# Attention sums transposed by VectorE straight from their PSUM bank, without ScalarE's copy in SBUF

## The reference

```python
h = x @ W1 + b1                                   # q, k, v, 16 heads of 8
w = einsum('bhqd,bhkd->bhqk', q, k) / sqrt(8)
w = softmax(w * mask - (1 - mask) * 1e6)
a = einsum('bhqk,bhkd->bhqd', w, v)
x = layernorm(x + a @ Wp + bp)
xr, xk = mu * x + (1 - mu) * x_prev               # one mu each
x = layernorm(x + sigmoid(xr @ W_r.T) * (square(relu(xk @ W_k.T)) @ W_v.T))
```

## Time and profile before

| | |
|---|---|
| median of 3 runs | 651.06 us |
| the profiled execution's own time | 650.12 us |
| its span, first to last instruction | 648.4 us |
| busy PE, DVE, ACT, POOL | 564.7, 550.0, 451.1, 413.6 us |
| L736, the copy to `osum`, 32 times | 18.7 us on ACT |
| L860, the transposition, 32 times | 22.4 us on DVE |
| one step in the steady part (from 290.32 to 325.64 us) | 35.32 us |

### The profile page before, as it was taken

One profiled execution on the slowest core, in us unless ns is written; L12 is line 12 of the kernel. 1 busy time (PEld: TensorE's weight loads), 2 busy tenths in 40 slices (PEclk: granted clock), 3 DMA queues, 4 the chain that ended last, 5 costly groups with the idle time before them and its releaser, 6 DMA issues.

```text
span 648.4 us, 17196 instructions
## 1 busy us (share of the span) xinstructions
PE 564.7 (87%) x6438; PEld 243.9 (38%) x6438; DVE 550.0 (85%) x1579; ACT 451.1 (70%) x878; POOL 413.6 (64%) x576
## 2 busy tenths in 40 slices
PE   3457888999999999999999999999999999997864
PEld 1122333444343534343443444343434344342333
DVE  1477789999999999999999999999999999894437
ACT  2102777777787878787878778787878787776831
POOL 4100425667778686767767786867777777757673
PEclk9999999999999999999999999999999999997965
DMA  4652262525355443726264545436362535410101
GB/s 169 116 148 51 84 135 77 140 52 149 85 148 101 134 101 116 134 85 135 51 168 81 149 103 147 95 125 116 117 126 64 133 66 148 85 37 3 33 17 33
DMA packets 70825, 65.78 MB, mean 101 GB/s; under 512 B 14357, under 2 KB 60502, under 8 KB 70742
## 3 DMA queue, kind: packets, MB, share of 16 engines
q1 hardware_dynamic: 70178, 64.22, 41.2%
q10 hardware_dynamic: 564, 0.46, 0.3%
HBM read 34.70 MB, written 29.88 MB: 100 GB/s over the span
## 4 chain that ended last, share of the span: by engine, by line
PE 38%; DVE 28%; POOL 14%; ACT 7%; issue 6%; DMA 5%; SPq 2%; DVEq 0%; POOLq 0%; ACTq 0%
DVE rowmax L813 16%; PE ops L606 12%; PE sps L579 8%; POOL probs L1021 6%; PE tps L541 5%; PE spare L502 4%; POOL scaled L1059 4%; PE sps L564 4%; ACT probs L730 3%; POOL mixed L1063 3%; PE spare L482 3%; PE spare L516 2%; DMA d_parts<-qk_parts 2%; DVE stats L819 2%; DVE attnT L876 2%
## 5 line engine op out<-in xcount | busy, mean ns | idle before, releaser
L813 DVE TENSOR_REDUCE rowmax<-sps 128x1 f32<-128x512 f32 (+7 forms) x1024 | 395.6, 444 | 36.0 <-PE sps L579 34.7
L730 ACT ACTIVATE probs<-tps 128x512 f32<-128x512 f32 x640 | 347.6, 598 | 98.0 <-PE tps L541 95.4
L1021 POOL TENSOR_SCALAR_AFFINE_SELECT probs<-probs 128x512 f32<-128x512 f32 x256 | 158.6, 637 | 172.8 <-ACT probs L730 172.2
L606 PE MATMUL ops<-probs,vop 128*32 128x384 f32 (+3 forms) x2048 | 173.7, 446 | 15.9 <-ACT osum L736 8.1
L579 PE MATMUL sps<-kop,qop 48*64 48x512 bf16 (+7 forms) x2048 | 130.0, 309 | 12.1 <-DMA kop<-d_parts 12.1
L541 PE MATMUL tps<-qop,kop 50*128 50x384 bf16 (+3 forms) x1024 | 126.7, 306 | 12.3 <-ACT probs L730 11.6
L564 PE MATMUL sps<-qmask,dup 64*128 64x128 bf16 (+1 forms) x640 | 69.8, 215 | 28.2 <-DVE rowmax L813 25.9
L541 PEld LDWEIGHTS tps<-qop,kop 50*128 50x128 bf16 x1024 | 34.2, 94 | 147.7 <-ACT probs L730 122.8
L606 PEld LDWEIGHTS ops<-probs,vop 128*32 128x32 f32 x2048 | 50.4, 109 | 79.5 <-issue 41.5
L579 PEld LDWEIGHTS sps<-kop,qop 48*64 48x64 bf16 x2048 | 43.0, 106 | 53.4 <-issue 21.7
L564 PEld LDWEIGHTS sps<-qmask,dup 64*128 64x128 bf16 x640 | 31.3, 94 | 75.2 <-DVE rowmax L813 70.7
(11 more groups left out here) (111 smaller groups left out, 501.0 us busy)
## 6 DMA issues: line engine op xcount, KB each, us to landing
qop<-d_parts SPq DMA_DIRECT2D x64, 192.0 KB, 4.5
kop<-d_parts SPq DMA_DIRECT2D x63, 192.0 KB, 5.0
d_parts<-qk_parts SPq DMA_DIRECT2D x15, 768.0 KB, 3.4
d_parts<-qk_parts SPq DMA_DIRECT2D x15, 512.0 KB, 4.6
d_parts<-qk_parts SPq DMA_DIRECT2D x17, 256.0 KB, 4.6
xT<-x_by_channel SPq DMA_DIRECT2D x16, 256.0 KB, 2.6
xres<-x SPq DMA_DIRECT2D x16, 256.0 KB, 3.5
out<-result SPq DMA_DIRECT2D x15, 256.0 KB, 2.5
```

The source lines that it names most:

```text
L606: last = nc.tensor.matmul(ops[32 * t:32 * t + 32, BLK * a:SEQ], vop[:, par, a, QUARTET * half + t, hh, :], probs[:, g % 2, i, off:off + w] ...
L730: nc.scalar.activation(probs[:, g % 2, i, :], tps[:, bank(n), :], ACT.Exp, scale=SCALE)\
L813: last = nc.vector.reduce_max(rowmax[:, par, QUARTET * half + i, a:a + 1], sps[:, bank(n), off:off + w], axis=AX_X)
L1021: last = nc.gpsimd.affine_select(out=v, in_=v, compare_op=ALU.is_ge, fill=0.0, base=0, pattern=[[0, QUARTET], [1, BLK]], channel_multiplie ...
```

## The change

ACT's copy, its semaphore and `osum` are taken out. DVE transposes out of the PSUM bank itself, one group sooner (groups 6 and 1), behind the first two reductions of the group; it waits for `pv_done`, and `pv` waits for `turned_done`. The reciprocal becomes a function of its own, `invert`, which stays in groups 7 and 2. For half 0, `divide` moves from group 8 to group 7, right behind the reciprocal; for half 1 it stays in group 3.

```diff
-        osum = sb("osum", [P, 2, SEQ])
...
-                    wait(pe, o_copied, 2 * batch + half)
+                    wait(pe, turned_done, 2 * batch + half)
...
-            def copy_o(n, half):
-                wait(act, turned_done, 2 * n + half - 1)
-                wait(act, pv_done, GROUPS * n + CHUNKS * (half + 1))
-                nc.scalar.copy(osum[:, half, :], ops[:]).then_inc(o_copied, 1)
...
-                        if place == 0 and tg == 1 and active("D", tb):
-                            copy_o(before("D", tb), 1)
-                        if place == 0 and tg == CHUNKS + 1 and active("T", tb):
-                            copy_o(before("T", tb), 0)
...
             def turn_sums(n, half):
 
                 m = 2 * n + half
-                wait(dve, o_copied, m + 1)
+                wait(dve, pv_done, GROUPS * n + CHUNKS * (half + 1))
                 wait(dve, attn_done, m)
-                nc.vector.transpose(turned[:].rearrange("q b s h d -> q (b s h d)"), osum[:, half, :])\
-                    .then_inc(turned_done, 1)
+                nc.vector.transpose(turned[:].rearrange("q b s h d -> q (b s h d)"), ops[:]).then_inc(turned_done, 1)
+
+            def invert(n, half):
+                m = 2 * n + half
                 wait(dve, turned_done, m + 1)
                 nc.vector.reciprocal(inv[:, half], turned[:, :, 1, :, 0]).then_inc(inv_done, 1)
...
+                    if tg == 1 and active("D", tb):
+                        turn_sums(before("D", tb), 1)
+                    if tg == CHUNKS + 1 and active("T", tb):
+                        turn_sums(before("T", tb), 0)
                     for _, use, n in ORDER[b, g, 0]:
                         spare_use(use, n)
                     if tg == 2 and active("D", tb):
-                        turn_sums(before("D", tb), 1)
+                        invert(before("D", tb), 1)
                     if tg == 3 and active("D", tb):
                         divide(before("D", tb), 1)
                         turn_back(before("D", tb))
                     if tg == CHUNKS + 2 and active("T", tb):
-                        turn_sums(before("T", tb), 0)
-                    if tg == CHUNKS + 3 and active("T", tb):
+                        invert(before("T", tb), 0)
                         divide(before("T", tb), 0)
```

More of the change, by code:

```diff
@@ L296, in block_program @@
         pv_done = sem("pv_done")
-        o_copied = sem("o_copied")
         turned_done = sem("turned_done")
```

## The result

The changed kernel takes 661.15 us, the median of 4 runs (658.49 to 663.85), against 650.67 for the kernel before beside it (4 runs, 649.69 to 652.81): a ratio of 1.016, with an interval of 1.011 to 1.021. It is slower, as forecast, but by 10.5 us where 2.95 were forecast, and it lies above the range. The profiled execution took 661.99 us, 11.87 more than that of before.

The account below looks back on a forecast made before the run. PE (33.50) and DVE (33.39 of 35.32 us per step) share the bound. 6.75 us lost, 2.80 and 1.0 gained: 651.06 + 2.95 = 654.0 us, range 649.0 to 657.5.

Parts of the forecast that it names:

- 15 x 0.45 = 6.75: Groups 6 and 7, half 0: group 8's first mask 0.45 us late in each of 15 steps, 6.75 us lost.
- `h` 0.51: DVE in groups 6 and 7: `h` behind the transposition takes 0.51 us, the same as before the change.
- ACT's copies: 32 copies of 0.58 us on ACT, which has 7 us to spare per step: removal counted at nothing beside the scores.
- The product in group 7: Half 0's product, moved from group 8, adds 0.41 us to DVE's work in group 7 and gives nothing back.
- PE's wait before `pv`: Group 6: `pv` starts 0.79 us later, behind the transposition; PE gets part back, leaving some 0.04 us.
- PE gets nothing back: Rival: PE sets the pace behind group 6, so 0.79 us are lost per step; 659.1 us, chance 0.07.
- Group 1 and 2: Half 1: group 2 is rid of the transposition, some 0.20 us gained per step, 14 times, 2.80 us.
- The price of the transposition: DVE transposing out of PSUM takes 0.70 us, as from SBUF, with 0.65 and 0.75 as the ends.
- the rival of a dearer one: Rival: the transposition out of PSUM takes 0.75 us, so both waits grow; 655.5 us, chance 0.13.
- Behind the last scores: After the last scores, DVE's transposition replaces the copy while DVE is idle: 1.0 us gained, bounds 0 and 1.0.
- the 0.62 us: Last batch's chain from `pv` over the transposition to its projection: shorter by a copy and a hand-over, some 0.62 us.

Follow-up runs that it names:

- `h_last`: The changed kernel with the second half of the layer norm (`h`) moved behind group 6's last two reductions; 653.89 us, ratio 1.003 to before.
- `masks_after_h`: The changed kernel with POOL's masks of group 6 waiting until `h` is done, DVE's order untouched; 652.41 us, ratio 1.000 to before.
- `idle_copy`: The changed kernel with an added ACT copy in group 6, in the old copy's place, that nothing reads; 657.69 us, one run.
- `product_g8`: The changed kernel with half 0's product put back from group 7 into group 8; 656.37 us, ratio 1.007 to before.
- `both_moved`: The changed kernel with half 0's product back in group 8 and `h` behind group 6's last two reductions; 650.5 us, ratio 0.999 to before.
- `turn_between`: The changed kernel with product back in group 8, `h` behind group 6's reductions, half 0's transposition between group 6's first two reductions; 650.8 us, ratio 1.000.

## Why the prediction was wrong

**The term that failed** is half 0's, "15 x 0.45 = 6.75". The first halves of the steps lost about 13.2 us in its place (the sum is below). The step in it that failed is "`h` 0.51": a duration was carried over from before to a place where it has another neighbour. `h` takes 1.14 there, which is 0.51 us per step as `h_last` and `masks_after_h` show it. The premise beside it failed too, by less: ACT's copies were counted at nothing, since nothing visible waited for ACT. What PE and DVE don't wait for still sets when POOL begins: the relief brought the masks 0.46 us forward, and 0.12 of the 0.51 us hang on it (`idle_copy`).

The Trainium skill has this rule ("SBUF — State Buffer", section "Who interferes with whom"): VectorE's `tensor_scalar` in its two-port mode and GpSimd exclude one another from a shared pair of ports; who comes first holds it for its whole instruction, and the other one stands still. The trace agrees on one side: `h` ends 0.08 or 0.09 us behind POOL's instruction in all 29 long rows, while the masks keep their length (1.23 us for two, before and after). No run shows in which mode `h` runs, or a mask that stands still for `h`. Nor do the starts alone decide who is held: in `idle_copy` 13 rows of `h` start 0.07 us ahead of the mask and are held all the same (0.79 to 0.80 us), while in the changed kernel one that starts 0.15 us ahead of it, at 117.69, is not (0.31).

**The product in group 7** was 0.41 and measured 0.33 (`product_g8`), or some 0.2 once `h` is out of the way (17.07 to 16.86). **PE's wait before `pv`** is there as forecast and is made up for, as forecast, but for at most 0.24 us, where the forecast had 0.04. The rival "PE gets nothing back" gave 659.1 us, nearest to the result, for a reason that `both_moved` excludes as the main one.

**Group 1 and 2**: -0.20 forecast, -0.27 to -0.28 measured, at the place and in the way described. **The price of the transposition**: 0.70 forecast, 0.704 measured; the rival of a dearer one falls. By the errata rule of the Trainium skill ("VectorE: DVE Perf Modes", TRN2 errata) it would have been an estimated 0.765; the trace doesn't show it.

**Behind the last scores** 1.0 us was forecast, and the time from the last `maxT` to the end is 0.96 shorter (60.63 to 59.67), but not by that working. At the end the transposition starts without the copy, and the product then waits (timelines of DVE and POOL after; of PE, DVE and POOL before):

```profile
636.38 0.72 DVE L849 STREAM_TRANSPOSE turned<-ops 128x512 f32<-128x512 f32 x1 [11.84 <-PE ops L604]
...
637.13 0.35 DVE L854 RECIPROCAL inv<-turned 128x32 f32<-128x32 f32 x1
...
637.46 1.26 POOL L1075 TENSOR_TENSOR xbias<-xres,bias_row 128x512 f32<-128x512 f32 x1
637.52 1.48 DVE L860 TENSOR_TENSOR attn<-turned,inv 128x256 f32<-128x256 f32 x1
...
639.03 0.71 DVE L867 STREAM_TRANSPOSE attnT<-attn 128x512 f32<-128x512 f32 x1
```

```profile
622.01 1.93 PE L606 MATMUL ops<-probs,vop 128*32 128x256 f32 x16 [3.03 <-POOL probs L1021]
...
625.09 1.27 POOL L1081 TENSOR_TENSOR xbias<-xres,bias_row 128x512 f32<-128x512 f32 x1
...
625.82 0.82 DVE L869 TENSOR_TENSOR attn<-turned,inv 128x256 f32<-128x256 f32 x1
...
626.66 0.71 DVE L876 STREAM_TRANSPOSE attnT<-attn 128x512 f32<-128x512 f32 x1
```

The product ends 0.28 us after POOL's `xbias` in both, so the 0.62 us are lost again: from the last `pv` (634.38 after) to `attnT` it is 4.65 us in both. The 0.96 came from 0.45 ahead of that `pv`, where 0.36 was forecast, and from 0.51 behind `attnT`, where PE's half-clock stretches lie otherwise than before; that the latter are the cause is argued only. That the total came out near 1.0 is thus in good part luck.

**The sum**, profile against profile, is 11.87 us: about +13.2 from half 0 (the first halves of all steps, 264.0 to 278.8 us, less 1.6 of half clock), -3.8 from half 1 (the second halves, 280.95 to 278.65, less 1.5 of half clock), -1.0 behind the last `maxT`, +0.3 at the start, and +3.1 that no step of the forecast has: three stretches at half clock, below.

## What to carry to other kernels

An instruction's duration from before holds only with its old neighbours. When a change moves an instruction, look what runs on the other engines at its new place; and when a change takes work off an engine with slack, follow what this engine releases, and look what the released work now stands beside. Split such a change by place before judging it: here one of its two halves alone is faster than either kernel (0.994 of before), and the other half alone carries the whole loss.

## What the runs showed of the hardware

DVE's `h` (fp32, SBUF to SBUF, 128x128) takes 0.30 to 0.35 us alone and up to 0.80 beside POOL's mask, which isn't lengthened. Not all of POOL's work does this: beside `max_parts` (0.22 and 0.24 us) the `h` of group 5 keeps to 0.33 to 0.36 us (28 rows). The product of two SBUF operands (0.42 alone) takes 0.82 before and 1.48 after beside `xbias`, and ends 0.28 us behind it both times; beside `scaled` it takes 0.41 before and 0.56 in `both_moved`, and isn't held to the end.

In the profile after, PE's granted clock falls to half (1.2 of 2.4 GHz) for three stretches of 3.41 us ahead of 600 us, at 333.7, 514.6 and 569.2 us, each as PE resumes after its 0.7 us before `pv`:

```profile
333.60 1.91 PE L604 MATMUL ops<-probs,vop 128*32 128x512 f32 x8 [0.71 <-DVE turned L849]
```

This `pv` takes 1.91 us instead of 1.06, and the half of a step that holds it is 0.8 us longer (18.41 against 17.58 above). The third costs some 1.5 us (19.83 us from group 0 to group 5, where `product_g8` has 18.29 without a fall), and all three some 3.1 us. Before had none until 590 us. The connection with the wait is open: most steps have the same wait and no fall. Of the other eight kernels, each with one profiled execution, three show one such fall between 70 and 590 us, also as PE resumes after 0.71 us before `pv` (`product_g8`, `idle_copy`, `turn_between`), and five none.
